# All scores of a batch of L2_xattn in one go in place of two and two, and the second half of its projections some slots sooner

## What is computed

```python
q = x @ Wq
kv = context @ Wkv
k, v = jnp.split(kv, 2, axis=-1)
q, k, v = (heads(q), heads(k), heads(v))
sim = jnp.einsum('bhid,bhjd->bhij', q, k) * SCALE
sim = jnp.where(mask[:, None, None, :], sim, max_neg)
sim = jnp.clip(sim, -5.0, 5.0)
attn = jax.nn.softmax(sim, axis=-1)
out = jnp.einsum('bhij,bhjd->bhid', attn, v)
out = out.transpose(0, 2, 1, 3).reshape(x.shape[0], x.shape[1], INNER)
return out @ Wo + bo
```

## Time and profile before

| | |
|---|---|
| median of 3 executions | 1715.98 us (1712.54 to 1717.97) |
| the profiled execution | 1713.31 us, span 1711.5 us |
| TensorE (PE) busy | 1607.3 us, 94% |
| VectorE (DVE) busy | 1392.4 us, 81% |
| ScalarE (ACT) busy | 1237.8 us, 72% |
| GpSimd (POOL) busy | 777.9 us, 45% |
| granted TensorE clock, mean | 0.975 |

### The profile page before, as it was taken

The page is one execution under the profiler, slowest core; times in us unless marked ns, Lnnn a source line. Parts: engine busy times, 40 slices in busy tenths (PEclk is TensorE's granted clock), DMA queues, the critical chain, the costliest instruction groups (busy, mean ns, idle before and its releaser), DMA issues. The chain is left out here.

```text
span 1711.5 us, 42342 instructions
## 1 busy us (share of the span) xinstructions
PE 1607.3 (94%) x14925; PEld 1210.5 (71%) x14925; DVE 1392.4 (81%) x4075; ACT 1237.8 (72%) x4825; POOL 777.9 (45%) x992
## 2 busy tenths in 40 slices
PE   8999999999989999789999999788899999999998
PEld 7886568999955556546667888556555677888877
DVE  6777887787899889888878787698899877777775
ACT  4557997666599999559993444386799767787775
POOL 2335882000166788357762111121677544445455
PEclk9999999999988799899999999889999999999999
DMA  9001000000000000000000000214000000111200
GB/s 303 1 2 40 2 2 2 2 2 2 2 2 2 2 2 2 1 1 2 2 2 2 2 2 2 95 56 191 2 2 2 2 2 14 50 50 51 68 21 26
DMA packets 16001, 43.28 MB, mean 25 GB/s; under 512 B 5680, under 2 KB 9008, under 8 KB 13872
## 3 DMA queue, kind: packets, MB, share of 16 engines
q1 hardware_dynamic: 15792, 40.58, 6.7%
HBM read 29.04 MB, written 11.53 MB: 24 GB/s over the span
## 5 line engine op out<-in xcount | busy, mean ns | idle before, releaser
L1894 POOL TENSOR_TENSOR a_probs<-a_probs,a_rinv 128x512 f32<-128x512 f32 (+1 forms) x288 | 272.4, 947 | 163.0 <-DVE a_rinv L1740 159.0
L1506 ACT ACTIVATE a_probs<-bank,a_negmax 128x128 f32<-128x128 f32 x896 | 326.4, 437 | 18.4 <-DVE a_negmax L1705 14.7
L1894 POOL TENSOR_TENSOR c_probs<-c_probs,c_rinv 128x512 f32<-128x512 f32 x192 | 200.2, 1043 | 187.3 <-DVE c_rinv L1740 184.1
L1506 ACT ACTIVATION_READ_ACCUMULATOR a_probs<-bank,a_negmax 128x1 f32 x896 | 240.8, 277 | 0.0
L1294 PEld LDWEIGHTS bank<-const,a_probs 128*128 128x128 f32 x1024 | 116.8, 145 | 115.0 <-issue 95.9
L1943 POOL TENSOR_TENSOR a_rstd<-a_ve,neg_half 128x1 f32<-128x1 f32 x128 | 70.6, 551 | 274.4 <-DVE a_ve L1793 273.2
L1294 PE MATMUL bank<-const,a_probs 128*128 128x128 f32 x1024 | 175.9, 291 | 2.2 <-DVE a_r L1771 1.0
L1709 DVE TENSOR_REDUCE a_negmax<-bank 128x4 f32<-128x512 f32 x192 | 130.1, 679 | 17.9 <-PE bank L1265 17.8
L1276 PE MATMUL bank<-state_t,w_L_ffn 128*128 128x128 f32 x1024 | 135.9, 276 | 0.0
L1747 DVE COPY a_probs_t<-bank 128x512 f32<-128x512 f32 (+1 forms) x192 | 118.4, 617 | 15.7 <-PE bank L1294 15.2
L1541 ACT ACTIVATE c_probs_t<-bank 128x512 f32<-128x512 f32 x176 | 105.4, 599 | 33.3 <-PE bank L1294 32.3
(11 more groups left out here) (304 smaller groups left out, 4328.5 us busy)
## 6 DMA issues: line engine op xcount, KB each, us to landing
space<-kept_halves SPq DMA_DIRECT2D x20, 512.0 KB, 4.4
kept_halves<-stage SPq DMA_DIRECT2D x6, 1024.0 KB, 4.6
w_L_ffn<-in_L_ffn SPq DMA_DIRECT2D x1, 3184.0 KB, 21.2
w_L_xattn<-in_L_xattn SPq DMA_DIRECT2D x1, 2050.0 KB, 8.9
kept_halves<-xq SPq DMA_DIRECT2D x2, 1024.0 KB, 4.1
kept_halves<-xqt SPq DMA_DIRECT2D x2, 1024.0 KB, 4.3
w_L_xattn<-in_L_xattn SPq DMA_DIRECT2D x1, 1536.0 KB, 8.2
ctx_t<-in_ctxT SPq DMA_DIRECT2D x1, 1024.0 KB, 11.5
```

Of the source, the lines that this page charges most:

```text
L1506: op = act.activation(p, bank_of("scores", n)[:, j * width:(j + 1) * width], ACT.Exp, scale=-1.0 if plan.masked_by_dve(s) else 1.0, bias=n ...
L1894: pool.tensor_tensor(p, p, along(rinv[:, n % PB, 0:heads], wide(kind) // heads), ALU.mult).then_inc(sems["norm_done"], 1)
```

## The change

```diff
-    "h64c": [("q0", 7, "act"), ("k0", 6, "act"), ("q1", 5, "act"), ("k1", 4, "act"), ("v0", 3, "act"), ("v1", 2, "act")],
+    "h64c": [("q0", 7, "act"), ("k0", 6, "act"), ("q1", 6, "act"), ("k1", 5, "act"), ("v0", 3, "act"), ("v1", 2, "act")],
...
+TOGETHER = {"h8": 2, "h8p": 2, "h8r": 2, "h64c": 4, "h64m": 2}
...
-            if stage == "scores" and kind in H8 + ("h64c", "h64m"):
-                now = at if i % 2 else max(now, at + 1)
+            if stage == "scores" and kind in TOGETHER:
+                now = at if i % TOGETHER[kind] else max(now, at + 1)
...
-                        if kind in H8 + ("h64c", "h64m") and i % 2:
+                        if kind in TOGETHER and i % TOGETHER[kind]:
                             return
...
                         if kind == "h64c":
-                            after_reader(pe, s, f"q{i // 2}")
-                            after_reader(pe, s, f"k{i // 2}")
-                            bank_free("scores", n + 1)
-                            for j in range(4):
-                                c = 2 * i + j
-                                for odd in range(2):
-                                    rows = slice(64 * odd, 64 * odd + 64)
-                                    mm = pe.matmul(bank_of("scores", n + odd)[:, j * S:(j + 1) * S], context_keys(s)[rows, c, :], Qs[rows, plan.ring(s, 2), c, :],
-                                                   start=True, stop=True)
-                                    if j == 3:
-                                        mm.then_inc(sems["scores_ready"], 1)
+                            for half in range(2):
+                                after_reader(pe, s, f"q{half}")
+                                after_reader(pe, s, f"k{half}")
+                                m = n + 2 * half
+                                bank_free("scores", m)
+                                bank_free("scores", m + 1)
+                                for j in range(4):
+                                    c = 4 * half + j
+                                    for odd in range(2):
+                                        rows = slice(64 * odd, 64 * odd + 64)
+                                        mm = pe.matmul(bank_of("scores", m + odd)[:, j * S:(j + 1) * S], context_keys(s)[rows, c, :], Qs[rows, plan.ring(s, 2), c, :],
+                                                       start=True, stop=True)
+                                        if j == 3:
+                                            mm.then_inc(sems["scores_ready"], 1)
                             return
```

## The result

The median after the change is 1715.83 us (20 executions, 1713.36 to 1722.56), beside 1714.44 us of the kernel before (20 executions, 1709.44 to 1717.97). The ratio is 1.0018, 95% interval 1.0011 to 1.0026: 3.1 us slower, with an interval of 1.9 to 4.5 us. (The ratio compares all executions and not the two medians: these differ by 1.4 us, the means, 1716.83 and 1714.08, by 2.8.) That lies within the 0.3% that was called "the same", and 1715.8 us is next to the 1715.7 forecast. But the sum behind the forecast was -0.3 us, and the interval excludes that. The time is right by luck, because the earlier median of three was high; what has to be explained is +3.1 where -0.3 was expected.

What follows compares the result with a forecast made beforehand. TensorE was taken to bound eleven periods of 12.70 us, VectorE the periods before them and the last. The terms -2.8 + 1.6 + 0.6 + 0.3 = -0.3 us, put on the median, gave 1715.7 us; range 1711.5 to 1720.

Steps and rivals of the forecast that it cites:

- Part 1: Eleven periods that TensorE bounds: fewer tile form changes and bank stalls, 12.45 us in place of 12.70, -2.8 us in all.
- Part 2: Periods that DVE bounds: two with k and v kept from an earlier layer, +1.6 us; the last, +0.6 us.
- Part 3: Beginning of the layer: q1 of batch 0 fills idle PE, more scores precede L2_attn's last output; +0.3 us.
- The late banks: Rival, chance 0.06: banks 4 and 5 handed on late stall every PE-bound period; slower, some 1729 us.
- The clock: Rival, chance 0.10: one half-clock stretch more or less, about 4 us either way; 1711.5 or 1720 us.
- a PEclk below 1 between 890 and 1090 us: Sign listed as showing the forecast wrong: TensorE's clock below full between those times; no size given.

Runs made afterwards that it cites:

- the projections alone: Kernel before with only q1 and k1 one slot sooner, scores still two and two: 1716.13 us, one execution.
- ends: Kernel before with scores in one go only in batches 0 to 3 and 15: 1720.79 us, ratio 1.0051.
- middle: Kernel before with scores in one go only in batches 4 to 14: 1711.46 us, ratio 0.9995; again 1709.85 us, ratio 0.9982.
- half filled: Changed kernel plus two matmuls nobody reads ahead of the outputs of batches 0, 1, 14 and 15: 1712.90 us, ratio 0.9999.
- the kernel with six fillers: Kernel before with scores in one go only in batches 4 to 14, plus six unread matmuls after the first loop's last output: 1712.83 us, ratio 0.9996.

## Why the prediction was right in its schedule and wrong in its sum

**Part 1, right.** Forecast 12.45 us and -2.8 in all; it is 137.13 / 11 = 12.47 and -2.6. The 0.19 us of form changes and the 0.04 left for the banks come apart in the experiment with the projections alone. The Trainium skill, "TensorE: Matmul & The Clock Gate", Part 2, would have given 0.05 us for the array to drain, by the estimate in the prediction; no run bears that out. The 0.19 of the rows stands: 12.66 - 12.47 is 0.19.

**Part 2, right in size.** Forecast 11.6 for the kept periods and 9.6 us for the last one; the window with a clock of 1.00 is 11.55, and the last scores to output take 1086.50 - 1076.89 = 9.61. DVE's reciprocal comes 2.69 us behind the scores' start (forecast 2.73), with the wait for the sums that was laid out, by DVE's timeline:

```profile
930.90 1.76 DVE L1732 RECIPROCAL a_inv<-bank 128x256 f32<-128x256 f32 x1 [0.68 <-PE bank L1325]
```

**Part 3, right.** Forecast +0.3, measured +0.38. It was taken as the middle between bounds of -0.7 and +0.9, so there is luck in it.

**The late banks** did not come: no PE row of a full period has a bracket. The second sums need bank 4, which the first reciprocal has read by 4.46 us behind the scores' start, and start at 5.38; the second values need bank 5, which the first product has read by 5.18, and start at 5.84. Covers of 0.9 and 0.7 us held; the prediction wrote 0.5 for the banks, where its own times give 0.9 and 0.6.

```profile
979.86 1.76 DVE L1732 RECIPROCAL a_inv<-bank 128x256 f32<-128x256 f32 x1 [0.68 <-PE bank L1325]
981.65 0.69 DVE L1735 TENSOR_TENSOR a_ot<-bank,a_inv 128x512 f32<-128x512 f32 x1
```

The Trainium skill, "Perfetto Trace Analysis", Matmuls, asks for groups in rotating banks; here the two pairs share theirs, and the full periods show no price. In the kept periods there is a small one: the second values start 0.63 us behind their sums (921.25 to 921.88) in place of 0.46, right behind the first product.

**The clock, the step that failed.** It stood among the rivals at 0.10, "one such stretch more or less, at 1.2 in place of 2.4 GHz, is worth about 4 us either way", and out of the sum. It is not of either sign. The list of what would show the prediction wrong did name "a PEclk below 1 between 890 and 1090 us", and that sign came; the rival even noted the "2 us of idle PE at a time" of the kept periods. The step that costed part 2 said "TensorE keeps up: it has 1 to 2 us to spare in each" and stopped there; but a ring longer by 0.79 us with the same work on TensorE is an idle stretch longer by 0.79: 1.45 became 2.21 us. And the q1 that moved away from ahead of the layer's first output had been a cover: 0.97 became 2.06. Of the moved step part 3 counted what it fills and not what it leaves empty. The size was off as well: 1.6 us per fall, 3.4 us at half clock, not 4. A term for parts 2 and 3, positive, from nothing to two falls (0 to +3.2 us), would have given the whole its sign.

What is shown: that the loss sits in the first and last periods (ends against middle), that it is the granted clock (windows of 0.87 beside one of 1.00 with the same instructions), and that the idle stretch brings it (half filled, with DVE's work unchanged; q1 sooner alone, with DVE's ring unchanged). Over all traces, the wait of 2.06 us had a fall behind it in 5 of 5 (three of the changed kernel, the ends, the projections alone), that of 2.21 in 3 of 4, and waits of 1.45 us and less at those two outputs in none of the other traces. What stays open is the layer's end. There the wait ahead of the last but one output grew from 0.88 to 2.23 us; a fall came right behind it in one of four traces (the ends), behind the last output's wait of 1.79 us, which the change did not touch, in the first trace after, the ends and the kernel with six fillers, and in none of the others. So the +1.6 us behind the last output in the trace after can't be put down to the change. The ratio fits two falls per execution, as the two other traces of the changed kernel have them, at the first outputs: -0.2 + 3.2 is +3.0. Why a wait of 2.2 us brings a fall in one execution and not in another stays open too.

## What to carry to other kernels

Where a change lengthens the chain of another engine in a stretch that this engine bounds, or moves TensorE's work out of a wait, TensorE's idle stretches lengthen by as much, and a clock term belongs into the sum with one sign. Ask of each wait how long it becomes at a piece, and look whether the profile already has a wait of that length and what clock stands behind it. An edit that pays in one regime and costs in the other can be made in the one alone: the middle batches give 3.4 us of layer, the ends take 2.9 back in schedule and more in falls. And a wait of known length can be filled by matmuls that nobody needs, if they are shorter than the wait: two of them took the loss away, four brought it back.

## What the runs showed of the hardware

- At the layer's beginning the clock falls for 3.4 us at a time (0.87 over 13.15 us), behind idle stretches of 2.06 to 2.21 us (8 of 9) and not behind those of 0.97 to 1.45; a fall costs 1.6 us. The length of the wait does not settle it alone: at the layer's end 1.79 us had a fall behind it in 3 of 11 traces, 2.23 us in 1 of 4. Behind the idle stretch of 3.44 us ahead of the second loop it is 7 to 10 us at half clock, and 3.4 us (0.88 over 14) where fillers had cut it to 0.92. The Trainium skill, "TensorE: Matmul & The Clock Gate", Part 1, says that the gate knows two rates only, half and full; the rows here agree: 16 output records take 2.0 or 3.7 us, and lie between the two only where a fall begins in their midst.
- The same instructions have their falls at other places in another execution (behind the first and the last output, or behind the first two), so one trace is a sample, and falls have to be counted over several. The mean clock of a dozen executions differed by 0.0011 between two sets of the same kernel, half of what two falls would be.
- A matmul of 128x512 in float32 is two records of some 0.44 us each (3.54 us for eight, up to the next start).
- A change between matmul tiles of 64 rows, of 32 columns and full ones costs 0.12 to 0.21 us by the earlier trace rows; the sum of these prices held to 0.02 us in a period of 12.5, and only their net of 0.19 was tested by an edit.
